# A gated recurrence feeding a mixture of experts: the high half of every second late weight split moves to ScalarE, and a few early steps change place

## What is computed

```python
h = scan(lambda prev, x_t: tanh(x_t @ Wx + b + prev @ Wh), cond, x)     # (2, 1024, 256)
# feed-forward on the 2048 states h, as rows of 256:
shared   = silu(h @ shared_w1.T) @ shared_w2.T                          # hidden width 1024
gates    = softmax over the top 2 of 8 of (h @ gate_w.T)
selected = sum over the 2 chosen experts e of gates[e] * (silu(h @ w1[e].T) @ w2[e].T)
out      = x + shared + selected
```

## Time and profile before

| | us |
|---|---|
| median of 3 runs (396.52 to 399.16) | 397.96 |
| profiled execution, its time | 401.65 |
| its span in the trace | 399.9 |
| TensorE busy in it | 371.8 (93%) |
| ScalarE, VectorE, GpSimd busy | 245.1, 220.8, 105.1 |

### The profile page before, as it was taken

One profiled execution on the slowest core, in us unless ns is written; L12 is line 12 of the kernel. 1 busy time (PEld: TensorE's weight loads), 2 busy tenths in 40 slices (PEclk: granted clock), 3 DMA queues, 4 the chain that ended last, 5 costly groups with the idle time before them and its releaser, 6 DMA issues.

```text
span 399.9 us, 9502 instructions
## 1 busy us (share of the span) xinstructions
PE 371.8 (93%) x2596; PEld 270.2 (68%) x2597; DVE 220.8 (55%) x469; ACT 245.1 (61%) x507; POOL 105.1 (26%) x107
## 2 busy tenths in 40 slices
PE   5979999995999989879999999999999999999991
PEld 4759999963676655646776666766667766667770
DVE  0189999966697989995433343333333333333310
ACT  3766876687376756536666566666666666666630
POOL 1000000000078778300013323332223333223332
PEclk9997999998899999999999999999999999999996
DMA  7999999304477989969789787877777877777982
GB/s 194 432 424 433 428 378 289 108 2 113 76 178 188 222 181 230 173 166 181 164 146 148 134 158 140 155 141 151 134 146 142 156 146 140 142 143 140 142 147 31
DMA packets 137437, 73.38 MB, mean 183 GB/s; under 512 B 115008, under 2 KB 134464, under 8 KB 136256
## 3 DMA queue, kind: packets, MB, share of 16 engines
q1 hardware_dynamic: 130544, 63.94, 65.3%
q0 software_dynamic: 6864, 9.08, 12.8%
HBM read 28.76 MB, written 16.46 MB: 113 GB/s over the span
## 4 chain that ended last, share of the span: by engine, by line
PE 74%; DVE 12%; issue 5%; DMA 3%; ACT 2%; SPq 1%; another core or an unknown queue 1%; POOL 1%; POOLq 0%; DVEq 0%; ACTq 0%
PE z L996 27%; PE py L1084 26%; PE z L1008 9%; PE z L981 4%; PE z L948 3%; PE px L1093 2%; DVE w_slots L517 2%; DVE w_slots L516 2%; DVE recurrence_w L580 2%; DVE space L580 2%; PE px L988 1%; DMA out<-space 1%; PE py L948 1%; DVE space L594 1%; PE z L961 1%
## 5 line engine op out<-in xcount | busy, mean ns | idle before, releaser
L1084 PE MATMUL py<-w_slots,space 128*128 (+1 forms) x1272 | 150.4, 276 | 7.9 <-DMA space<-recurrence_w 4.3
L1084 PEld LDWEIGHTS py<-w_slots,space 128*128 128x128 f16 x1272 | 124.8, 99 | 26.8 <-DVE space L594 5.1
L996 PE MATMUL z<-w_slots,x_hi 128*128 (+1 forms) x424 | 126.2, 379 | 1.4 <-issue 1.2
L850 ACT ACTIVATE space<-z,tile_scales 128x512 f32<-128x512 f32 x106 | 72.5, 684 | 56.2 <-PE z L996 36.4
L442 POOL DMA_INDIRECT out<-space x37 | 57.5, 1554 | 173.7 <-issue 106.0
L996 PE MATMUL z<-w_slots,x_lo 128*128 (+1 forms) x212 | 80.3, 379 | 0.0
L580 DVE SCALAR_TENSOR_TENSOR recurrence_w<-space,tile_scales,recurrence_w 128x512 f16<-128x512 f32 x54 | 40.4, 750 | 64.5 <-ACT recurrence_w L855 35.4
L580 DVE SCALAR_TENSOR_TENSOR space<-space,tile_scales 128x512 f16<-128x512 f32 x52 | 39.0, 750 | 61.6 <-ACT space L855 53.3
L996 PEld LDWEIGHTS z<-w_slots,x_hi 128*128 128x128 f16 x424 | 41.5, 98 | 42.5 <-issue 3.5
L517 DVE SCALAR_TENSOR_TENSOR w_slots<-w_slots,w_scale 128x1024 f16<-128x1024 f32 x36 | 46.2, 1285 | 1.3
L855 ACT ACTIVATE recurrence_w<-space,tile_scales 128x512 f16<-128x512 f32 x54 | 39.0, 723 | 9.6 <-ACT space L850 3.3
(11 more groups left out here) (114 smaller groups left out, 268.0 us busy)
## 6 DMA issues: line engine op xcount, KB each, us to landing
w_slots<-weights SPq DMA_DIRECT2D x9, 2048.0 KB, 30.3
sorted_rows<-pad_row SPq DMA_DIRECT2D x1, 5031.0 KB, 62.0
space<-sorted_rows SPq DMA_DIRECT2D x39, 129.0 KB, 2.4
space<-x_rows SPq DMA_DIRECT2D x16, 128.0 KB
out<-space SPq DMA_DIRECT2D x16, 128.0 KB
space<-x_cols SPq DMA_DIRECT2D x1, 1024.0 KB, 8.3
space<-recurrence_w SPq DMA_TRANSPOSE x54
space<-space SPq DMA_TRANSPOSE x52
```

Of the source, the lines that this page charges most:

```text
L850: nc.scalar.activation(hidden[:, half], Z[p][h][:], ACT.Silu, scale=tile_scale(g, 0)).then_inc(hidden_ok, 1)
L996: last = nc.tensor.matmul(Z[p][h][:], x[:, p, k], weight(f, k * HID + h * BANK, BANK, part), start=k == 0 and x is x_hi and part == 0, sto ...
L1084: last = nc.tensor.matmul(PY[p][:, 0:D], hiddenT[:, p, low, q], weight(f, MATRIX + q * D, D, part), start=q == 0 and not low and part == 0 ...
```

## The change

- SyncE: the two first loads of `x_res`, and the wait for `up_mm` ahead of them, stand behind turn(0) and no longer ahead of it.
- TensorE: the prefix sums stand inside down(0), between its high and its low part, and no longer behind it.
- VectorE and ScalarE: in stages 6 to 13 the first of the two late pieces gets its high part from ScalarE (`nc.scalar.mul`, at the end of ScalarE's stage, when `split_ok` has reached c); VectorE waits for `high_ok` and writes the low part. The second piece stays whole on VectorE. `shared_y` stands ahead of both.
- GpSimd: in `add` the register load and the wait for the neighbour come ahead of the wait for `y_ok`.

```diff
-            sp.wait_ge(up_mm, 3 * HALVES)
...
-            for g in range(2):
-                sp.dma_start(x_res[:, g], x_tiles[g]).then_inc(x_res_in[g], 16)
...
             for g in range(TILES):
                 turn(g, g % 2)
+                if g == 0:
+                    sp.wait_ge(up_mm, 3 * HALVES)
+                    for n in range(2):
+                        sp.dma_start(x_res[:, n], x_tiles[n]).then_inc(x_res_in[n], 16)
...
                 waited(idx_ok, t + 1)
-                waited(y_ok, t + (TILES + 1))
-                if t >= 2:
-                    waited(added[(t - 2) % RING], outs_of(t + 2))
                 if 1 <= t <= RING:
                     waited(added[(t - 1) % RING], outs_of(t + 3))
                 elif t:
...
+                    neighbour = pool.value_load(neighbour_out[0:1, t:t + 1], min_val=16, max_val=outs_of(SLOT_TILES + RING))
+                    waited(added[(t - 1) % RING], neighbour)
+                if t >= 2:
+                    waited(added[(t - 2) % RING], outs_of(t + 2))
+                waited(y_ok, t + (TILES + 1))
...
+                if high_by_act:
+                    dve.wait_ge(high_ok, (c - LATE_WIDES) // 2 + 1)
+                else:
+                    link(nc.vector.tensor_scalar(high, whole, scale, None, ALU.mult))
                 nc.vector.scalar_tensor_tensor(low, whole, scale, high, ALU.mult, ALU.subtract).then_inc(split_ok, 1)
...
-                    else:
-                        split_upto(ahead_wides + 4 * WIDES * (g - 5) // (TILES - 8))
                 if g >= AHEAD:
                     shared_y(g - AHEAD)
+                if SPLIT_FROM <= g < TILES - 2:
+                    c = LATE_WIDES + 2 * (g - SPLIT_FROM)
+                    split(c, high_by_act=True)
+                    split(c + 1)
...
+                if SPLIT_FROM <= g < TILES - 2:
+                    c = LATE_WIDES + 2 * (g - SPLIT_FROM)
+                    whole, high, low, scale = wide(c)
+                    act.wait_ge(split_ok, c)
+                    nc.scalar.mul(high, whole, scale).then_inc(high_ok, 1)
...
             def down(g, p, n, f):
...
                 for low in range(2):
+                    if low and isinstance(g, int) and g == 0:
+                        prefix_sums()
```

More of the change, by code:

```diff
@@ L96 @@
 LAST = FFNS - 1
+SPLIT_FROM = 6
+LATE_WIDES = BOUND_BATCHES[4][0] * WIDES
 def build(nc, x_cols, x_rows, h0_cols, wx, wh, bias, weights, gate_cols, out):
@@ L223, in build @@
         bound_ok, found = sem("bound_ok"), sem("found")
-        bound_all_ok, split_ok = sem("bound_all_ok"), sem("split_ok")
+        bound_all_ok, split_ok, high_ok = sem("bound_all_ok"), sem("split_ok"), sem("high_ok")
         x_res_in = [sem(f"x_res_in{u}") for u in range(2)]
@@ L272, in weight, with wide @@
             return w_split[:, bass.ds(f * (2 * WCOLS) + (2 * c + part) * WIDE + start, n)]
+        def wide(c):
+            f, m = c // WIDES, c % WIDES // (WIDES // 2)
+            high, low = (w_split[:, (2 * c + part) * WIDE:(2 * c + part + 1) * WIDE] for part in range(2))
+            return w_slots[:, 2 * c + 2:2 * c + 4].rearrange("p s c -> p (s c)"), high, low, w_scale[:, f, m:m + 1]
         @block.sync
@@ L506, in find_scales, with split @@
                                                     DOWN_UNSCALE, w_pow[:, start:end, 1], ALU.mult, ALU.mult))
[L508 to L513, removed]
+            def split(c, high_by_act=False):
+                whole, high, low, scale = wide(c)
                 if c:
                     dve.wait_ge(split_ok, c)
-                link(nc.vector.tensor_scalar(high, whole, scale, None, ALU.mult))
+                if high_by_act:
+                    dve.wait_ge(high_ok, (c - LATE_WIDES) // 2 + 1)
+                else:
+                    link(nc.vector.tensor_scalar(high, whole, scale, None, ALU.mult))
                 nc.vector.scalar_tensor_tensor(low, whole, scale, high, ALU.mult, ALU.subtract).then_inc(split_ok, 1)
@@ L701, in _ @@
             route_choice()
-            ahead_wides = BOUND_BATCHES[4][0] * WIDES
             for g in range(1, TILES):
@@ L717, in _ @@
                     if g == 3:
-                        split_upto(ahead_wides)
+                        split_upto(LATE_WIDES)
                         find_scales(4)
@@ L1075, in up, with prefix_sums @@
                     up_half(p, f, h, up_mm)
+            def prefix_sums():
+                pe.wait_ge(picked_ok, 1)
+                for n, m in enumerate((before, ones)):
+                    last = nc.tensor.matmul(PX[:, (n + 1) * P:(n + 2) * P], m[:], picked.rearrange("p t e -> p (t e)"),
+                                            start=True, stop=True)
+                last.then_inc(prefix_mm, 1)
             def down(g, p, n, f):
@@ L1127, in _ @@
                 down(g, g % 2, 16 * (g // 2 + 1), SHARED)
-                if g == 0:
-                    pe.wait_ge(picked_ok, 1)
-                    for n, m in enumerate((before, ones)):
-                        last = nc.tensor.matmul(PX[:, (n + 1) * P:(n + 2) * P], m[:], picked.rearrange("p t e -> p (t e)"),
-                                                start=True, stop=True)
-                    last.then_inc(prefix_mm, 1)
             def iteration(t, u, n, n_in, up_next=True, fetch=True):
```

2 lines of the change are left out of this document (removed).

## The result

| | before | after |
|---|---|---|
| median, us (6 runs each) | 398.37 (396.52 to 399.17) | 393.25 (392.38 to 396.26) |
| profiled execution, its time | 401.65 | 394.0 |
| its span | 399.9 | 392.3 |

The ratio is 0.9888, interval 0.9847 to 0.9929: 5.1 us faster between the medians, where 11.4 were forecast. 393.25 lies above the range.

What follows compares the result with a forecast made beforehand. TensorE bounds from 179.86 us on; between 90 and 180 us VectorE is full, with one half-clock TensorE stretch. down(13) 12.2 us earlier, less 1.7 for stops, plus 0.9 for adds: 11.4 off, 386.6 us; range 382.3 to 391.5.

Steps and rivals of the forecast that it cites:

- Tile 0's transposes: SyncE's queue: high transpose at 90.25 instead of 94.32, so down(0) starts at 93.4, 3.8 us earlier.
- sums inside down(0): TensorE: prefix sums done by 96.0; VectorE's later work and `routed` come 6.6 us earlier, up(3) 6.3 us earlier.
- The rival of the clock: At down(0): the clock falls anyway, so the 2.6 us expected from full clock are lost; 389.2 us, chance 0.08.
- High part on ScalarE: Late stages: one multiply of 1.1 us moves to ScalarE; VectorE loses 0.78 us eight times, its stage falling to 5.37.
- The rival of the lock step: Late stages: VectorE-ScalarE meetings cost what the multiply saves, pace stays 6.15 us; 390.5 us, chance 0.14.
- The plan: Stages 2 to 9 at TensorE's 5.64 us, down(9) at 144.5, down(13) at 167.6, 12.2 us earlier.
- Sorting: GpSimd's scatters: 3.3 us a tile, ending by 157.2, row copies at the limit from tile 14; nothing counted.
- The rival that said this: Sorting holds the stages back: row copies wait for landings, down(13) at 171 to 172; 388.6 us, chance 0.17.
- Output ahead of the splits: VectorE's late stages: down no longer waits for the stage's end, so its 0.77 us wait goes.
- The last link: From the end of VectorE's stage 12 through tile 13's transpose, store and sorted-row load to down(13): 7.0 us.
- The stops that I took 1.7 us off for: ScalarE's unnamed row-copy stops, 3.14 us once, now holding VectorE too: none to three expected, half of one deducted.
- The adds: GpSimd's final adds: early register load shortens the end chain by 0.9 us, bounds 0 and 1.4.

Runs made afterwards that it cites:

- e1: Kernel before with the early moves alone (tile 0's transposes ahead of the x loads, prefix sums inside down(0)): 393.53 us, ratio 0.9838.
- e14: Kernel before with the early moves alone, a second time: 393.08 us, ratio 0.9858.
- e17: Changed kernel with six sorting buffers in place of four and the output behind the splits again: 388.58 us, ratio 0.9734.
- e11: Kernel before with only the high part of every second late piece on ScalarE, output behind: 397.87 us, ratio 0.9929.
- e7: Changed kernel with a ring of six sorting buffers in place of four: 393.57 us, ratio 0.9844.
- e10: Kernel before with only the shared output ahead of the late splits: 402.72 us, ratio 1.0066.
- e13: Changed kernel with the output behind the splits again, a second time: 391.48 us, ratio 0.9828.
- e9: Changed kernel once more, unedited: 394.3 us, ratio 0.9869 to the kernel before.
- e4: Kernel before with only the early register loads of GpSimd's adds: 399.14 us, ratio 0.9983.
- e6: Changed kernel with four buffers for x in place of two, loads two stages earlier: 392.03 us, ratio 0.9821.
- e8: Changed kernel with four buffers for x and six for sorting: 391.3 us, ratio 0.9806.
- e18: Changed kernel with four buffers for x and six for sorting, a second time: 388.14 us, ratio 0.971.
- e5: Changed kernel with the output behind the splits again; ScalarE still makes the high parts: 393.94 us, ratio 0.9863.
- e2: Kernel before with ScalarE's high parts and the output ahead of the splits, no early moves: 400.89 us, ratio 1.0027.
- e12: Changed kernel with four x buffers, six sorting buffers and the output behind the splits: 394.93 us, ratio 0.986.

## Why the prediction was wrong

Three things that the prediction named as signs of being wrong came: starts of down over 6 us apart (7.01, 8.24, 6.88), row copies that stand long, and a clock that falls.

*Tile 0's transposes, sums inside down(0), clock there: right.* The first transpose goes out at 88.58, 0.1 us after its high part ends, down(0) follows at 2.9, at full clock. e1 and e14 give 6.5 and 5.7 us. The rival of the clock has no part in it at this place.

*High part on ScalarE: right in mechanism and in VectorE's time.* 1.15 us where 1.1 was taken, VectorE's stage 5.35 where 5.37 was (e17, from 156.79 to 162.14). In e17 VectorE waits 0.16 to 1.74 us in stages 6 to 10 and TensorE stays at 5.64 to 5.79 a stage. The rival of the lock step falls with it. What this is worth is less sure: 2.8 us alone (e11), and 1.7 from down(0) to down(13) between the profiles of e14 and e17 (76.8, 75.1). The plan counted 5.9 us after down(1), against a profile in which down(2) to down(9) came 6.2 us apart with stops of ScalarE between them. In e14, without such stops, down(1) to down(7) came 5.65 apart with all high parts still on VectorE.

*Sorting: the step that failed.* "By this count it is at the limit from tile 14 on. I count nothing for it." The count took 3.3 us a tile from a profile in which VectorE held the stages at 6.15 us, and 2.3 for the landing, for which no row stands. In the changed kernel the 16 tiles took 57.4 us (102.9 to 158.9 and one more scatter), 3.6 a tile, while TensorE delivers one every 2.8. The median scatter went from 1054 to 1206 ns, and from issue to landing it took 3.9 us, up to 5.8. A ring of four doesn't hide that there: row copies wait 5.8 us in three, from ScalarE's stage 8 on, TensorE stands 3.31 us for them, and the halved clock adds 1.67. So down(7) to down(10) took 22.13 us for a planned 16.9, most of the 6.0 that the stretch to down(13) missed. e7, with six buffers and no other edit, takes it in 16.50. The rival that said this was priced at 2 us; between the profiles of e7 and the changed kernel it is 3.6 to down(13). The wait and where it acts are shown. Its price in the median is not: e7 has 0.9844 and the changed kernel 0.9888 and 0.9869, 1.0 to 1.8 us with intervals that overlap.

The forecast of 11.4 us fits e17 (11.0), which has neither this wait nor the output ahead of the splits. The longer ring alone, e7, has 6.3. So the sorting is not the only loss, and that e17 comes so close may be in part luck: its gain over e14 is 1.7 us in that stretch of the profiles and 4.5 between the medians, which are of different sessions.

*Output ahead of the splits: wrong in sign.* The prediction asked what is late next for TensorE (the low transpose) and not what is late next for VectorE. The order shows `x_res_in0` in the output's wait. The output now comes some 3.4 us earlier in the stage, x rows land 2.4 to 3.1 us after a load that SyncE issues one stage ahead, and the splits are queued behind. The changed kernel has three such waits ahead of down(13), 4.2 us, where the kernel before has none (6 and 6.8 us in all against 2 and 1.9). Only the last, 1.09 us at 160.53, lies on the chain that ends at down(13): after the first TensorE didn't stand, and during the second the multiply was late anyway. The other cost is the one long stand at the last link, after which down(13) took 1.33 us more (4.11 - 2.78). e10, the output ahead alone, is 2.6 us slower, with an interval of 1.7 to 3.6, and its profile has only the second cost.

*The last link: 7.0 forecast, 7.5 came* (164.24 to 171.72), and 7.0 in e13 and e17.

*The stops that I took 1.7 us off for* don't come in the changed kernel's profile. In e9, the same kernel again, there is one of 1.51 us.

*The adds:* 0.9 forecast, 0.7 from e4 with an interval around nothing. The chain at the end shows 0.6 less.

*The rule of the Trainium skill* (SBUF — State Buffer, Who interferes with whom) made me put the sorting rival lower: eight `tensor_scalar` fewer on VectorE should spare GpSimd. No run here shows that. The scatters' median rose to 1206 ns and 1230 in e17; in one session it was 1068 in e13 with eight fewer and 1026 in e14. These records don't rule out that it helped and closer traffic ate it.

*The level.* 3.7 us between the profiled execution and the median were carried over, and in the changed kernel that difference is 0.75. How far the later start of tile 0 in the profile before (1.73 us) belongs to it is not shown, since only one execution of each has a trace.

What stays open: what the wait for scatters costs in the median, since no session has the same kernel with four and with six sorting buffers but for e6 and e8, and e8 had unnamed stops; how the 3 us between e8 and e18, the same kernel, arise (their intervals don't overlap, and e8's profile has the unnamed stops and e18's none); and why e5 has a median of 393.94 with a profiled execution of 389.14.

## What to carry to other kernels

When a change lets one engine run faster through a stretch, recount every ring of buffers in it at the new pace, with the producer's interval against the consumer's and the landing, before counting the gain; a ring "at the limit" needs a price. When an instruction is moved ahead on its engine, list every semaphore it waits for and ask of each when it comes, not only who waits for the instruction. And where a change gives half of its sum, look for the stretch in which no engine is full.

## What the runs showed of the hardware

**A halved clock is the price of gathering waits.** Between down(1) and down(13) of these profiles TensorE went on at 2.4 GHz after each stand of 1.22 to 1.86 us, and at 1.2 GHz after stands of 2.07, 2.30, 2.35, 2.38, 2.74, 2.88, 2.89, 2.90 and 3.04; after 2.26 it fell once (e9, stage 9) and once not (e2). The down product behind such a stand took 4.06 to 4.45 us in place of 2.78.

**The same code has another clock from one execution to the next.** 0.62, 0.81 and 1.00 between 27 and 36 us in kernels that are the same up to there. Tile 0's high part starts at 87.75 to 91.09 us in the twenty profiles, and this clock alone doesn't order them.

**Unnamed stops of ScalarE at row copies** come in the profiles of the kernel before, e1 to e4, e6 and e8 to e12, 0.9 to 5.3 us long and most between 112 and 131 us, and in none of e5, e7, e13 to e18 and the changed kernel's first. All of e1 to e4 and of e9 to e12 have them, none of e13 to e18, and two of the four of e5 to e8. So they go more with the session than with the kernel, though not with it alone. In e12 the matmuls that ScalarE waits for are in the records at 112.72, while the trace has the signals of down(3), of these transposes and of both halves of up(5) all between 117.89 and 118.09. TensorE's signals came late together; what held them isn't shown. Where VectorE holds the pace the medians don't show their cost (e1 has them and e14 doesn't, 0.9838 and 0.9858), but the profiles do: 80.9 us from down(0) to down(13) in e1 and 76.8 in e14.
